# A recurrent two-layer block on one core: the order in which five engines are handed the steps of a round, laid out anew

## What is computed

```
xn = _layernorm(x)
s = _L0_attn_ref(xn, ...)            # 4 blocks: quaternion products, spectral filter, MLP
g = _silu(_L0_ffn_ref(xn, ...))      # 8 experts, top 2
x = x + s * g
xn = _layernorm(x)
s = _L1_attn_ref(xn, ...)            # windowed attention, 16 heads
g = _silu(_L1_ffn_ref(xn, ...))      # 32 experts in 16 pairs, top 4, and a shared one
x = x + s * g
```

## Time and profile before

| | |
|---|---|
| runs of the kernel | 5060.56, 5062.42 and 5063.08 us, median 5062.42 |
| span of the profiled execution | 5060.7 us |
| one middle round, 15 of them | 303.8 us |
| TensorE busy | 4509.6 us, 89% of the span |
| VectorE busy | 4181.3 us, 83% |
| ScalarE busy | 3166.3 us, 63% |
| GpSimd busy | 2078.6 us, 41% |
| mean granted TensorE clock | 0.945 of 2.4 GHz |
| table loads on ScalarE | 584 |
| DMA | 30 GB/s mean |

### The profile page before, as it was taken

One profiled execution on the slowest core, in us unless ns is written; L12 is line 12 of the kernel. 1 busy time (PEld: TensorE's weight loads), 2 busy tenths in 40 slices (PEclk: granted clock), 3 DMA queues, 4 the chain that ended last, 5 costly groups with the idle time before them and its releaser, 6 DMA issues.

```text
span 5060.7 us, 75398 instructions
## 1 busy us (share of the span) xinstructions
PE 4509.6 (89%) x20080; PEld 2766.1 (55%) x20208; DVE 4181.3 (83%) x8946; ACT 3166.3 (63%) x6063; POOL 2078.6 (41%) x2033
## 2 busy tenths in 40 slices
PE   5679899898998989899998998989889998998989
PEld 3345555564555655555564555655555564555655
DVE  5689798888979889798888979889798888979853
ACT  2447666675766757666675766757666675666745
POOL 2234344443434444344443434444344443434423
PEclk8779999999999999999999999999999999999979
DMA  4001101111101101101111101101101111101100
GB/s 120 15 26 28 29 25 30 28 30 29 26 26 28 34 22 28 29 25 30 28 29 29 26 26 27 35 21 29 29 25 30 27 30 29 26 25 28 35 19 20
DMA packets 144530, 149.37 MB, mean 30 GB/s; under 512 B 27748, under 2 KB 107932, under 8 KB 143960
## 3 DMA queue, kind: packets, MB, share of 16 engines
q1 hardware_dynamic: 144088, 144.19, 10.9%
HBM read 22.45 MB, written 4.19 MB: 5 GB/s over the span
## 4 chain that ended last, share of the span: by engine, by line
PE 51%; DVE 27%; issue 14%; ACT 4%; POOL 1%; SPq 1%; DVEq 1%; DMA 0%; ACTq 0%; POOLq 0%
PE bT L1302 8%; DVE acc L952 8%; DVE tmp L952 6%; PE bA L1174 5%; PE bC L1359 5%; PE bU L1352 5%; PE bG L1345 4%; PE bA L1264 4%; PE bT L1314 4%; PE bT L1158 3%; DVE tmp L814 3%; PE bT L1287 2%; PE bA L1255 2%; DVE hu L1139 2%; PE bT L1327 2%
## 5 line engine op out<-in xcount | busy, mean ns | idle before, releaser
L644 POOL TENSOR_TENSOR s_h<-s_h,ge 128x512 f32<-128x512 f32 x512 | 730.2, 1426 | 1303.7 <-ACT ge L654 1052.9
L776 ACT ACTIVATE s_h<-bG 128x512 f32<-128x512 f32 x528 | 314.0, 595 | 709.9 <-DVE hu L1139 421.6
L952 DVE TENSOR_TENSOR acc<-acc,tmp 128x512 f32<-128x512 f32 x768 | 696.9, 914 | 4.2
L603 POOL TENSOR_TENSOR veA<-mvA,epsT 128x2 f32<-128x2 f32 x290 | 112.9, 389 | 1315.8 <-DVE mvA L807 1315.8
L1359 PE MATMUL bC<-hu,w_d 128*128 128x512 f32 x1056 | 582.3, 634 | 10.0 <-DVE hu L1139 9.6
L952 DVE TENSOR_TENSOR tmp<-comps 128x512 f32<-128x512 f32 x768 | 582.1, 766 | 5.8
L1302 PE MATMUL bT<-Kk,Q 64*128 64x256 f32 (+1 forms) x2048 | 545.5, 388 | 31.2 <-DVE y L1121 7.3
L753 ACT ACTIVATE probs<-bT,nmax 128x256 f32<-128x256 f32 x1024 | 413.6, 474 | 229.7 <-DVE nmax L1100 225.8
L1100 DVE TENSOR_REDUCE nmax<-bT 128x2 f32<-128x512 f32 x512 | 350.2, 685 | 194.4 <-PE bT L1302 192.3
L1314 PEld LDWEIGHTS bT<-V,probsT 128*128 128x128 f32 x3584 | 433.4, 194 | 79.6 <-issue 36.0
L1139 DVE TENSOR_TENSOR hu<-bU,s_h 128x512 f32<-128x512 f32 x528 | 360.8, 683 | 108.7 <-PE bU L1352 74.5
(11 more groups left out here) (201 smaller groups left out, 9650.8 us busy)
## 6 DMA issues: line engine op xcount, KB each, us to landing
rot<-raw SPq DMA_DIRECT2D x1024, 64.0 KB, 2.0
comps<-comps SPq DMA_DIRECT2D x384, 120.0 KB
x_ld<-in_L_attn_x SPq DMA_DIRECT2D x66, 128.0 KB, 2.2
comps<-comps SPq DMA_DIRECT2D x384, 8.0 KB
out<-O SPq DMA_DIRECT2D x16, 256.0 KB, 2.7
w_a<-in_L_attn_W_qkv SPq DMA_DIRECT2D x1, 1536.0 KB, 14.8
w_fc<-in_L_attn_fc_w SPq DMA_DIRECT2D x1, 1024.0 KB, 8.3
w_g<-in_L_ffn_w_gate SPq DMA_DIRECT2D x1, 1024.0 KB, 5.9
```

The costliest lines, as they stand in the source:

```text
L644: nc.gpsimd.tensor_tensor(s_h[:, :], s_h[:, :], ge[:, :], ALU.mult).then_inc(weighed, 1)
L776: nc.scalar.activation(s_h[:, :], bG[:, :], ACT.Silu).then_inc(silu, 1)
L952: V_.tensor_tensor(dst, i0, i1, op).then_inc(ham[h], 1)
```

## The change

All five strings of `ORDER` are written anew; nothing else is touched. The same steps are handed out, with the same operations, waits, tiles and buffers. On TensorE 126 of 347 steps keep their place, on ScalarE 110 of 309, on VectorE 114 of 315, on GpSimd 46 of 99, on SyncE 26 of 43; the mean step moves 1.3, 1.3, 1.6, 0.8 and 0.6 places, the farthest 13. SyncE's string and the first line of TensorE's in the diff:

```diff
-    "pe": "uuuaauabbauubtuubutuuutuutuuutuuuuttuuuuttataututtutatuauutauauauatbuuuabauattauubtbutubtbtubtbu"
...
+    "pe": "uuuuaabatbuaububuutuutuutuutuuuuuttuuuttutauauttuuttuutuaatuaatuauaubuuuabauauuatubbtubtbtbttbuuu"
...
-    "sp": "aababtttbtaattabbtbtaatatbbbttttaabbattabbt",
+    "sp": "aabbttabttaattabbtbtaaattbbtbtttaababbabttt",
```

More of the change, by code:

```diff
@@ L126 @@
 ORDER = {
-    "pe": "uuuaauabbauubtuubutuuutuutuuutuuuuttuuuuttataututtutatuauutauauauatbuuuabauattauubtbutubtbtubtbu"
-          "utuuubuttbuubtttauautbutatatttatatattatututuutttuautuabubatuatuububtttbububutbuuttubttbuubtattbu"
-          "autuautttuauattutauauatatttbutuubtbttuatabubuattttbtbtbtbtauttuttbtubuubtbuutttatttattubututtuub"
-          "ttuutuutuuutuuuutuuuaututatbuuttbtuutattabuabtbuababtabtbta",
-    "act": "uuaaaubaababaaaabtaubbuabbbbbuttauutubuuttbtuttttttuatuataaauuuaaaaataaaaatbuatbtbabbuuttauttbtb"
-           "tububtbtubbbbbbattabtaattattttttuubuttauaauaaataaaaaubtbutbtabbuuatttbttbtbubutbbbtbbbbutubtbaau"
-           "atautaattttttuuttababubtuatabtbtabtttaaatttaaatbtbubbubbabbbbtbutabbatttbutttttuuttuuuuuutrtuutt"
-           "ttttuatabtbabababtabu",
@@ L135 @@
-    "dve": "abatubatabuaaabauababauababauabatauababautabtatabtbuabrbtbubtbrbaautbarbbuaabraaauataratatababau"
-           "abatauataabatuaabtarbbbtbbbbtbtbtbbatbuabbtatbubtbabbaubaaaaaaauaatatabbauatbtaaatbatbauatbbbabb"
-           "ubtbbbbbbbtbtbbttuabatbbatubttaattbbtbtutaaaaabbtaaubbtbbatbabttbabtautbbrabtaubababatubabaubaru"
-           "batbtratbutabrbatbutttbtbaa",
-    "pool": "aubtuababuuaututtuuattubtuauabaauubtubtuabtbuauttauabtuubtatubbtabuuaubtttuaatbatabubbtbuuttutuu"
+    "pe": "uuuuaabatbuaububuutuutuutuutuuuuuttuuuttutauauttuttuutuaatuaatuauaubuuuabauauuatubbtubtbtbttbuuu"
+          "tututububtbtbttuuauatuttutatatatatattatuttuuttuatuautabuabuuutbuutbubtbubtutbtuttuubttbuubtbttau"
+          "atuttauuttuauatuttauauatattutububtabttutaubatbttbtbtabutbttuttuttbtubutbutbuttuattattubtutbuttuu"
+          "ttuutuutuutuuttuutuutuutauuutabubututttabuabtabtababuabtbta",
@@ new lines @@
+    "act": "uuaaabaabbuaaaabaabbtbauubabbutttbuuuubtttututttttbuutaataaauuuaaaaauaaaaabbtabtbtbtuuaatttubtbt"
+           "tbbubbuttbbtbbbutaataattattttttbubuuattaaauuaaaaaauabtubbtbtbautauttttbtbtbbuubttbbbbbuttbabbuta"
+           "uatauaattttttuuttbaaabubttbattbabtaautattttaaabttbbuubbatbtabbbbbtutbabtbutttttuuttuuututtuutruu"
+           "ttttutabtabababtababu",
+    "dve": "abtaubtaabuaaabaauaaauababauaatauaattbubabbatabbturbabtbtbbubbrbaauabtbrubaabruaaaraaaababtattua"
+           "abatauatabatabaautrabbbbtbbbbbbtbbttatuabbattbubtbabbaubaaaauaaaaaabtbtaattbauaatabatbatuabbbabt"
+           "bubbbbbbbttbubtbabtabtabtbubtatatbttbtbutaaabtabauatbbababaabbatbabttbtuabtabtrubabturbatbuababt"
+           "taubabtaburbabrabtutttbtbaa",
@@ L140 @@
+    "pool": "uabtaaubuaubtututuuattubtuauaabauubtutubtabtbutauaaubauttubtubbtauubaubtattatutabbubatbbutututuu"
             "uab",
-    "sp": "aababtttbtaattabbtbtaatatbbbttttaabbattabbt",
+    "sp": "aabbttabttaattabbtbtaaattbbtbtttaababbabttt",
 }
```

## The result

The changed kernel takes 4988.74 us (median of 4 runs, 4957.77 to 4998.97), against 5062.09 us before: 73 us or 1.45% less by the medians; over all runs of both kernels the ratio is 0.9845, 95% interval [0.9814, 0.9876]. TensorE's mean granted clock was 0.945, 0.938, 0.936 and 0.935 in the executions of 4957.8, 4980.3, 4999.0 and 4997.2 us. The kernel before scattered by 2.5 us, this one by 41.

The account below looks back on a forecast made before the run. No single engine was taken as the bound; VectorE or TensorE binds by stretch. Per round -2.5 - 1.8 + 1.9 = -2.4 us, times 15 = -36, giving 5026 us; range 4983 to 5078, likeliest case 5010 to 5045.

Parts of the forecast that it names:

- the case called more: Rival: no new load on the path, TensorE's clock up in the first stretch; 4982 us, or 4998; chance 0.16.
- VectorE is full and stays so; six more dependent neighbours cost 0.7 us: From block 0's second-half `hart` to block 1's `ln2_T`: VectorE sets the pace; steps of one half in sequence add 0.7 us.
- the gain is given back: Rival, about nothing: squeezed idle time puts more VectorE product steps beside GpSimd, lengthening them; 5062 us, chance 0.20.
- The first stretch: Round's start to the second half's `hart` of block 0: 5.2 us idle removed, 1.1 us dependent steps added, net -4.1.
- I take all four idle times as gone: VectorE's waits before block 0's second-half `hart`, for `up 4`, `proj`, `S 0 3` and `hidden 8`, vanish: 5.2 us a round.
- V 3 over the crossing: `V 3` moves behind the second half's `ln2_T` of block 1, where TensorE has no spare time: +0.9 us a round.
- The fourth stretch: From `down 23` to block 3's second-half `hart`: two maxima +1.2, `k` turn earlier -0.8, table loads +1.9; together +2.3 us.
- the +1.2 for two maxima: Maxima of `S 7 1` and `S 7 2` now precede block 3's second-half `hart`, adding 1.2 us on VectorE.
- Table loads: ScalarE loads 41 tables a round instead of 37, 1.30 us each; one and a half on the path: +1.9 us.
- The rival built on them: Slower: table loads on ScalarE between `S 7 0` and `S 7 2`, and near `S 0 1`, take the path; 5081 us, chance 0.22.
- The fifth: Behind block 3's second-half `hart`, TensorE-bound: `down 30`, `S 7 3` and a `PT` now run earlier, saving 2.2 us.
- First and last round: Rounds with only half of the streams; 0 for both together, bounds -5 and +5 us.

Follow-up runs that it names:

- -2.1 alone: New order on all five engines only for the steps from the round's start to the second half's `hart` of block 0, against the kernel before: 5028.2 us, ratio 0.9921.
- the second stretch alone: New order only from the second half's `hart` of block 0 to its `ln2_T` of block 1, against the kernel before: 5066.5 us, ratio 1.0004.
- the two orders with the new later stretches alone: Kernel before with the new order only in the last two or last three of a round's five stretches, a few steps differing: 5097.9 and 5103.2 us.

## Why the prediction was wrong, point by point

The sign was right, the size was not: -36 forecast, -73 measured, and -105 in the profiled run. The measured time lies in the wide range (4983 to 5078), outside the forecast's own (5010 to 5045), and in the case called more (4982 to 4998), whose chance was 0.16. That case's reasons do not carry it: the clock of the first stretch did rise, from 0.85 to 0.92 as the mean of eleven rounds, but the stretch gave 2.5 us and not more than the 4.1 of the forecast, and whether a load lies on the path no run tells. What goes beyond the forecast is the second stretch, for which neither case had a gain of this kind.

**The step that failed** is "VectorE is full and stays so; six more dependent neighbours cost 0.7 us". It took VectorE's busy time as fixed, and priced the second stretch at +0.7 us where -4.3 came. It was 74.7 us in that stretch, and 65.6 after, because products and norms (136 and 40 operations a round) lay partly beside GpSimd's, and the order changes that. From the records of twelve middle rounds, each VectorE record put to the GpSimd record that it overlaps most: before, 84 of the 136 products lay beside none of GpSimd's and took 681 ns on the mean; 22 beside the unit product took 1274, 12 beside the rotary product 1248, 6 beside the rotary sum 1640. After, 93 lay beside none; the unit product stretched 20, to 1019. These means mix the three widths of the products; those of 128x512 alone took 683 ns beside nothing, and 1191, 1125 and 1619 beside the three. The prediction had this very effect in its hands, 1.28 us against 2.34, and made of it only a rival on the side of loss ("the gain is given back"). It asked for a rise of VectorE's 261.6 us a round as the sign of being wrong, and never for a fall. They fell to 236. The Trainium skill, "SBUF — State Buffer", section "Who interferes with whom", would have said which operations to count: one of VectorE with two inputs in SBUF contends with a GpSimd instruction that reads SBUF, a `tensor_scalar` in a two-port mode contends with GpSimd, and one with at most one input there and no two-port mode doesn't. The trace agrees in each form: in before L952 (128x512), L935 and L1096 go from 683, 286 and 679 ns to 1191, 592 and 951 beside the unit product, and L814 from 337 to 1272 beside the rotary sums; L1139, L1100 and L1111 keep 683, 684 and 424 ns beside whatever of these they meet.

**The first stretch** (-4.1) was mis-sized: -2.5 in after, -2.1 alone. `hart`'s 1.49 us went as said, and the 6.9 us behind it were at full clock in nine rounds of eleven. But the wait for `hidden 4` didn't: it grew from 1.70 us on VectorE to 2.38, since `weight 4` on GpSimd comes behind a rotary product that waits for its rows. "I take all four idle times as gone" was the over-reach; one of them came back larger. VectorE's timeline in after:

```profile
1812.45 0.69 DVE L1139 TENSOR_TENSOR hu<-bU,s_h 128x512 f32<-128x512 f32 x1 [2.38 <-POOL s_h L644]
```

**The second stretch** is dealt with above: -4.3 for +0.7.

**V 3 over the crossing** (+0.9): right in place and sign, +1.1 in after. With the second stretch alone 2.5 us are lost in the third.

**The fourth stretch**: +2.0 for +2.3, but not for its reasons. The 4.04 us at `OT 6` did go, as forecast. VectorE, which I called full there, had 7 to 8 us less to do, so the +1.2 for two maxima doesn't show. What the stretch paid instead is TensorE: it is busy in 58.2 of 61.0 us, waits at `prep_T` and `route0`, and is granted 0.89 of its clock for 0.97 before (0.91 as the mean of eleven rounds). The agreement of the sum is luck here.

**Table loads** (+1.9): the count was right, 648 in all. The price is not shown: no run has a load on the path, at +1.9 us a round or any other. Taking 62 away made the kernel slower, but moved two SiLUs later with them, so that run prices the move and not the loads. The rival built on them (5081 us) has something like its symptom in the two orders with the new later stretches alone, which lose 34 and 39 us; that the loads are the cause there is not shown.

**The fifth** (-2.2): -2.7. **First and last round** (0): of the 104.8 us of the profiled span, 97.1 lie between the second and the last start of `gate 2` (fourteen rounds, 6.9 each), 2.3 ahead of them and 5.4 behind, where the last middle round lies as well; right, within the bounds of 5 us.

**What would show it.** 301.4 us a round was forecast, 297.3 came; VectorE's idle time in the first stretch was to fall from 11 us to 6, and stays at 11.7 in the round shown (65.85 - 54.19), 14.1 as the mean of eleven: by the prediction's own mark it was wrong there; "no wait of 4 us at `OT 6`" and "648 table loads" held.

## What to carry to other kernels

Before pricing a new order, split each VectorE form's mean duration by what GpSimd runs beside it: a mean well above what the form takes alone (717 for 337 ns here) is time that an order can give back without removing work; with the order of before, all of it that the unit and rotary products take was worth 439 us, against 36 forecast from waits. A kernel with GpSimd's reads taken out (same steps, about the same length) prices it in one run. And an order that is better with that cost in it can be worse without it (256 us of 4624 here), so a change that moves the operations off GpSimd, or shortens them, is to be tried on both orders: with GpSimd's reads taken out, the old one is the faster here.
